# Cross-attention on Trainium2: six scalings of probabilities per batch moved from VectorE to ScalarE

## The reference

```python
q = ln_lat @ Wq                                        # ln_lat: 256 tokens of x, normalised
kv = jnp.concatenate([xn, ln_lat], axis=1) @ Wkv       # 256 context rows and the 256 tokens: 512 keys
k, v = jnp.split(kv, 2, axis=-1)                       # 16 heads of 64
weight = jnp.einsum('bhld,bhnd->bhln', q * scale, k * scale)
weight = jnp.where(full_mask[:, None, None, :], weight, neg)
weight = jax.nn.softmax(weight, axis=-1)               # exp(w - max) / sum
out = jnp.einsum('bhln,bhnd->bhld', weight, v)
return out.transpose(0, 2, 1, 3).reshape(b, l, heads * dim_head) @ Wout
```

## Time and profile before

| | us |
|---|---|
| median of 3 runs | 2608.73 |
| profiled execution, its own time | 2615.02 |
| its span in the trace | 2613.3 |
| cross-attention (15 passes and the last one) | about 659 to 2045 |
| between equal instructions of two neighbouring passes (Exp of unit 4 at 1015.34 and 1101.98) | 86.64 |
| TensorE busy | 2348.9 (90%) |
| VectorE busy | 1916.7 (73%) |
| ScalarE busy | 1707.6 (65%) |
| GpSimd busy | 1038.8 (40%) |

### The profile page before, as it was taken

One profiled execution on the slowest core, in us unless ns is written; L12 is line 12 of the kernel. 1 busy time (PEld: TensorE's weight loads), 2 busy tenths in 40 slices (PEclk: granted clock), 3 DMA queues, 4 the chain that ended last, 5 costly groups with the idle time before them and its releaser, 6 DMA issues.

```text
span 2613.3 us, 62103 instructions
## 1 busy us (share of the span) xinstructions
PE 2348.9 (90%) x18056; PEld 1962.6 (75%) x18056; DVE 1916.7 (73%) x5340; ACT 1707.6 (65%) x4373; POOL 1038.8 (40%) x1096
## 2 busy tenths in 40 slices
PE   6899998885999999999999999999999479999990
PEld 5777787774777777777777777777776379999990
DVE  6788888875766776677767776677666378888866
ACT  5787888773665666666666666676667266767652
POOL 4454545535333333333334233423341234444424
PEclk9999999997999999999999999999999689999995
DMA  7555555551000000000000000000000377777766
GB/s 194 131 134 126 123 124 128 127 122 41 18 18 9 9 17 17 9 9 17 17 9 9 16 17 9 9 16 17 14 3 9 101 221 236 237 232 236 230 220 201
DMA packets 161045, 224.40 MB, mean 86 GB/s; under 512 B 33920, under 2 KB 127744, under 8 KB 160640
## 3 DMA queue, kind: packets, MB, share of 16 engines
q1 hardware_dynamic: 151008, 202.42, 27.9%
q0 software_dynamic: 9664, 20.53, 2.3%
q10 hardware_dynamic: 224, 0.00, 0.0%
HBM read 140.15 MB, written 24.01 MB: 63 GB/s over the span
## 4 chain that ended last, share of the span: by engine, by line
PE 64%; DVE 4%; issue 3%; POOL 2%; DMA 1%; ACT 0%; SPq 0%; DVEq 0%; POOLq 0%; ACTq 0%
PE x_proj L1827 18%; PE x_av L1926 9%; PE x_score L1897 8%; PE y_bank L2513 8%; PE x_ptb L1909 8%; PE h_bank L2499 8%; PE x_out_sum L1864 4%; PE x_proj L1811 1%; POOL x_rstd L1317 1%; PE x_proj L1802 1%; PE xt_bank L2481 1%; DVE x_stat L1569 1%; DMA w_s<-w 0%; DVE wox L1636 0%; POOL rstd L2282 0%
## 5 line engine op out<-in xcount | busy, mean ns | idle before, releaser
L1440 ACT COPY x_pt<-x_ptb 128x512 f32<-128x512 f32 x512 | 272.3, 583 | 188.5 <-PE x_ptb L1909 187.9
L1636 DVE CUSTOM_DVE_ANT_0 wox<-x_score,x_mask_add 128x512 f32<-128x512 f32 x352 | 239.4, 683 | 173.4 <-PE x_score L1897 122.4
L1434 ACT ACTIVATE wox<-wox,x_low 128x512 f32<-128x512 f32 x352 | 251.7, 718 | 107.1 <-DVE x_low L1636 103.7
L501 ACT ACTIVATE prob<-prob,low 128x128 f32<-128x128 f32 (+1 forms) x512 | 228.7, 450 | 111.4 <-DVE low L728 110.2
L1337 POOL TENSOR_TENSOR x_k_lo<-x_whole,x_k_hi 128x512 fp32r<-128x512 f32 x128 | 164.7, 1287 | 337.8 <-ACT x_k_hi L1481 336.1
L1926 PE MATMUL x_av<-x_pt,x_vx 128*64 128x256 f32 x2048 | 249.9, 386 | 0.6 <-ACT x_ox_hi L1448 0.6
L1615 DVE COPY x_whole<-x_proj 128x512 f32<-128x512 f32 x192 | 130.7, 687 | 124.0 <-PE x_proj L1827 121.5
L2307 ACT ACTIVATE h_t<-h_bank,b_s 128x256 f32<-128x256 f32 x312 | 130.7, 470 | 108.2 <-PE h_bank L2499 98.3
L1647 DVE TENSOR_SCALAR wox<-wox,x_rden 128x512 f32<-128x512 f32 x352 | 200.4, 611 | 0.6
L2499 PE MATMUL h_bank<-xg_hi,w_hi 128*128 128x256 f32 x624 | 177.7, 285 | 22.4 <-DVE xg_lo L2372 21.0
L1926 PEld LDWEIGHTS x_av<-x_pt,x_vx 128*64 128x64 f32 x2048 | 136.1, 137 | 80.9 <-issue 12.5
(11 more groups left out here) (303 smaller groups left out, 7980.4 us busy)
## 6 DMA issues: line engine op xcount, KB each, us to landing
w_s<-w SPq DMA_DIRECT2D x156, 512.0 KB
k_parts<-k_hi SPq DMA_DIRECT2D x128, 128.0 KB, 2.4
q_parts<-q_hi SPq DMA_DIRECT2D x128, 128.0 KB, 2.4
k_parts<-pos_parts SPq DMA_DIRECT2D x128, 64.0 KB, 2.4
k_parts<-k_lo SPq DMA_DIRECT2D x64, 128.0 KB, 2.4
q_parts<-q_lo SPq DMA_DIRECT2D x64, 128.0 KB, 2.4
w_s<-expert_rows SPq DMA_DIRECT2D x16, 512.0 KB, 4.8
b_s<-b SPq DMA_DIRECT2D x39, 128.0 KB
```

Source lines behind the costliest of these rows:

```text
L501: ins = nc.scalar.activation(s, s, ACT.Exp, bias=low[:, u, c:c + 1], scale=-1.0, accum_out=den[:, u, c:c + 1])
L1434: nc.scalar.activation(slot, slot, ACT.Exp, bias=low[:, u:u + 1], scale=-1.0, accum_out=den[:, u:u + 1]).then_inc(exp_ready.sem, 1)
L1440: nc.scalar.copy(pt[:, u % PX_RING, :], ptb[u % 2][:, :]).then_inc(pt_taken[u % 2].sem, 1)
L1636: dve.tensor_tensor_reduce(prob_slot(u), score[u % 2][:, :], mask_add[:, :], -X_SCALE, 3.0e38, ALU.add, ALU.min, low[:, u:u + 1]).then_inc ...
```

## The change

For the pairs 0 to 5 (`SHARED = 6`) of every batch VectorE scales only the first unit and raises `rden_ready`, which now counts two for each pair: one for the reciprocal, one for this scaling. ScalarE waits for both, scales the second unit with an ACTIVATE (Copy, scale from `rden`) and raises `prob_ready` in VectorE's place. It does so in step i for pair i - 1, behind the two Exps of the step and ahead of the copies of transposed blocks. For pairs 6 to 15 VectorE scales both units as before (its reciprocal then raises `rden_ready` by two); at pair 6 it first waits until `prob_ready` has been raised for pair 5.

```diff
+    SHARED = 6
...
-        rden_ready = signal("rden_ready", HEADS)
+        rden_ready = signal("rden_ready", 2 * HEADS)
...
+            def probabilities(b, h):
+
+                act.wait_ge(rden_ready.sem, rden_ready.at(b, 2 * h + 2))
+                u = 2 * h + 1
+                slot = prob_slot(u)
+                nc.scalar.activation(slot, slot, ACT.Copy, scale=rden[:, u:u + 1]).then_inc(prob_ready.sem, 1)
...
                     if i < HEADS:
                         for c in range(TC):
                             exps(b, 2 * i + c)
+                    if 1 <= i <= SHARED:
+                        probabilities(b, i - 1)
                     if 2 <= i < HEADS + 2:
                         for half in range(2):
                             take_transposed(b, 2 * (i - 2) + half)
...
             def one_over_sum(b, h):
                 dve.wait_ge(exp_ready.sem, exp_ready.at(b, 2 * h + 2))
-                dve.reciprocal(rden[:, 2 * h:2 * h + 2], den[:, 2 * h:2 * h + 2]).then_inc(rden_ready.sem, 1)
+                dve.reciprocal(rden[:, 2 * h:2 * h + 2], den[:, 2 * h:2 * h + 2]).then_inc(rden_ready.sem, 1 if h < SHARED else 2)

             def probabilities(b, h):
-                dve.wait_ge(rden_ready.sem, rden_ready.at(b, h + 1))
-                for u in (2 * h, 2 * h + 1):
+                dve.wait_ge(rden_ready.sem, rden_ready.at(b, 2 * h + (1 if h < SHARED else 2)))
+                if h == SHARED:
+                    apart(prob_ready, prob_ready.at(b, SHARED))
+                for u in (2 * h,) if h < SHARED else (2 * h, 2 * h + 1):
                     slot = prob_slot(u)
                     ins = dve.tensor_scalar(slot, slot, rden[:, u:u + 1], None, ALU.mult)
-                ins.then_inc(prob_ready.sem, 1)
+                if h < SHARED:
+                    ins.then_inc(rden_ready.sem, 1)
+                else:
+                    ins.then_inc(prob_ready.sem, 1)
```

## The result

The changed kernel takes 2617.5 us (median of 9 runs, 2614.75 to 2624.94) against 2608.73 (here 9 runs too, 2605.86 to 2612.84): ratio 1.0035, 95% interval [1.0024, 1.0046], 9 us slower. The forecast was 2608.6 with a range of 2602 to 2617, and no change as the likeliest outcome.

The account below looks back on a forecast made before the run. TensorE was taken as the bound, with at most 2.2 us a pass to win in steps 2 to 6. 15 passes at +0.02 are +0.3, less 0.4 in the last pass, -0.1 us: 2608.6 us, range 2602 to 2617.

Parts of the forecast that it names:

- VectorE's side: Pairs 0 to 5: one of two scalings leaves VectorE, each freeing 0.40 us; scores of pair 4 come 0.37 us earlier.
- ScalarE's price: Six ACTIVATEs added to ScalarE in each pass, each taken to add 0.62 us to its queue.
- c: What one added 128x512 scaling adds to ScalarE's queue: taken as 0.62 us, with ends at 0.47 and 0.72.
- The sum of the queues: One pass followed through steps 2 to 6: net at the scores of pair 7 between -0.01 and +0.04 us, taken +0.02.
- the new wait ahead of pair 6: In VectorE's queue ahead of pair 6's scaling, for ScalarE's scaling of pair 5: free, with 0.4 us spare.
- step 7 and on: From step 7 of a pass TensorE has no wait, and nothing more is gained or lost.
- 0.62 late: Steps 2 and 3: TensorE's transposes of pair 1 start 0.62 us later; scores of pair 4 still gain 0.37 us.
- The first (the relief holds): Rival, chance 0.18: ScalarE's queue doesn't bind in steps 4 to 6, TensorE keeps 0.46 us a pass; 2601.4 us.
- The second (ScalarE as the bound): Rival, chance 0.22: ScalarE becomes the bound, c over 0.81; transposes of pair 5 0.67 us a pass later; 2618.6 us.

## Why the prediction was wrong

**VectorE's side was right.** Counted from the logits' matmuls in front of them, the scores of pair 3 come after 66.16 us (1121.43 to 1187.59) as they did before (66.16, 1036.51 to 1102.67): pair 0's scaling is worth nothing, and pair 1's doesn't move them. From there the scores of pair 4 come 0.39 earlier (0.37 forecast).

**ScalarE's price was right.** c was taken as 0.62. ScalarE's timeline in the short pass of after, steps 4 and 5:

```profile
1195.01 0.71 ACT L1443 ACTIVATE wox<-wox,x_rden 128x512 f32<-128x512 f32 x1
...
1195.62 1.04 ACT L1448 COPY x_pt<-x_ptb 128x512 f32<-128x512 f32 x2
...
1199.57 0.71 ACT L1443 ACTIVATE wox<-wox,x_rden 128x512 f32<-128x512 f32 x1
...
1200.19 1.04 ACT L1448 COPY x_pt<-x_ptb 128x512 f32<-128x512 f32 x2
```

The copies start 0.61 and 0.62 after the scalings in front of them. The trace agrees with the Trainium skill here ("ScalarE: Activation LUTs", section "What ACT_TABLE_LOAD costs"): 709 to 714 ns measured against an estimate of 706 by its formula, and 0.61 in the queue by both. The copies of pair 3 start 12.60 us after the scores of pair 3 (1200.19 less 1187.59), and my sum had them at 12.60 (1115.27 less 1102.67). No table load was added, and ScalarE never waited for VectorE's half in the short passes; in six of the seven long ones it did once, 0.25 us for a scaling that took 1.59 on VectorE instead of 0.48.

**The sum of the queues was right.** Net of a pass +0.02 forecast; measured 86.63 where it had been 86.63. Also right: the new wait ahead of pair 6 costs nothing, and step 7 and on give no wait.

**The step that failed** is the one that put the transposes of pair 1 "0.62 late" and priced this only as a delay that VectorE's hold on the scores of pair 4 would have covered. That is its whole price in the queues, but I had TensorE's granted clock in the same table at 1.00 and gave no term to it. The wait ahead of these transposes grew from 0.46 to 1.08 us, another wait of 0.58 lay just in front, and in 7 of 14 intervals TensorE's clock fell to 0.50 shortly after it had come back, for 3.4 us, which cost 0.87 us of the pass. Filling the wait takes the loss away (ratio 0.9997), making it in the kernel before brings a loss of the same kind (1.0018): for both directions this is shown. Whether the wait of 0.58 in front has a part in it isn't, as every kernel here has it; and why the clock falls in one pass and not in the next, with equal queues, stays open. The Trainium skill ("TensorE: Matmul & The Clock Gate", section "Part 1: The HAM clock gate") says that a gate lets half or all of the array's clock through by how busy TensorE has been, with nothing in between. The traces agree: 0.50 or 1.00, and the values between in the tables above are means over a stretch with both. For the fall it names an idle TensorE, and further down short idle times between groups of matmuls that come often enough. Here the clock fell where TensorE had worked between two waits, and the page alone would not have told whether 1.08 us is too long.

In the trace the term is 7 x 0.87 = 6.1 us. The measured 9 us are more than that; how many passes had such a stretch in the timed runs isn't seen, and up to 15 x 0.87 = 13 us could be had from it. The clock points that way: the profiled execution, 2615.86 us, has a mean granted clock of 0.962 over the whole kernel. The nine runs have 0.958 to 0.962; the four with 0.961 or 0.962 took 2614.8 to 2617.5 us, the five below 2617.4 to 2624.9. By an estimate from these rows one stretch (3.4 us at half clock in 2615) lowers the mean by 0.00065, so the median of 0.960 would have some three stretches more than the profiled one, 2.7 us. Where those runs lost their clock isn't seen, so the part of the loss over 6 us is argued and not shown.

The profiled executions hid this: 2615.0 before, 2615.9 after, 0.8 apart. The first logits come at 689.96 us before and at 685.70 after, and the last two lie 50.35 and 47.69 apart: 4.3 and 2.7 us that the execution after gained in work that the change doesn't touch or hardly touches. The granted clock differs there as well: from 2003 to 2009 us, in the last pass, it is 0.50 before and 1.00 after. The pass lengths are the measure, not the two spans.

**The rivals.** The first (the relief holds) had the right mechanism and a term too small: 0.46 a pass, and the kernels with pairs 1 and 2 have 0.66. I took about 1.04 us, the time to the end of the eight transposes, as TensorE's step from them to the next scores, where it moves on after 0.97 (1193.47 to 1194.44), and so put the scores of pair 5 at 0.46 instead of 0.63 earlier. For six scalings it needed a c under 0.39; with only pairs 1 and 2 moved it holds at 0.61, so which pairs are shared decides it more than the price. The second (ScalarE as the bound) happened for its queue alone in the kernel without pair 1 (+0.43 a pass), at c = 0.61 and not over 0.81, because there VectorE's gain is missing that pays for it. The changed kernel was slower without either: that the second rival's 2618.6 lies nearest to the measured time is chance. The rule of the Trainium skill ("ScalarE: Activation LUTs", section "Rules for kernel authors": "Use VectorE, not ScalarE" for a multiplication) came out on the right side for another reason; with pairs 1 and 2 moved and the wait filled, going against it gains 0.4%.

## What to carry to other kernels

When a change makes the bounding engine wait longer at one place and less at another, the sum of the waits isn't the whole price: look at TensorE's granted clock in the stretch behind the longer wait, pass by pass, and treat a wait that grows as this one did (0.46 to 1.08 us) as a risk even where it is covered. If such a wait can't be avoided, a few matmuls that nothing reads can be put into it: here they cost nothing and kept the clock. And when an engine is full in some steps only, move work to it in the steps before those: two scalings in the right place, with the wait filled, gained about what six had lost.

## What the runs showed of the hardware

The same queue, to some hundredths of a microsecond, had TensorE at half clock in every second pass and at full in the others. Where TensorE had waited 0.58 and then 1.08 us, the clock fell in some of the passes; where it had waited 0.58 and then 0.46 (with 0.93 more behind) or 0.4, in none. The fall came up to 0.7 us after TensorE had come back from the second wait. A half-clock stretch lasted about 3.4 us in each case and cost 1.53 us a pass where nothing hid it (without the filler, pairs 1 and 2), 0.87 where a later wait took up the rest. An instruction that only copies and scales takes 0.61 us of ScalarE's queue for 128x512 (1195.01 to 1195.62), about as long as Exp before its accumulator read begins (0.63).
